# Three pieces moved in the hand-written order of a two-layer transformer kernel's first part

## The reference

```python
h = tok(x, W, b)                                  # patches -> 256 channels
h = concatenate([h, table[x_txt]], axis=1)
h = h + attention(layernorm(h))                   # q.k via a merged wq'wk matrix, causal, softmax, times v
h = h + ternary_down(gelu(ternary_up(rmsnorm(layernorm(h)))))
h = h + recurrent_block(layernorm(h))             # part b
h = h + experts(layernorm(h))                     # part c
```

## Time and profile before

| | us |
|---|---|
| median of 3 runs | 1094.04 (1093.84 to 1098.66) |
| the profiled execution's own time | 1092.31 |
| its span (first to last instruction) | 1090.5 |
| busy TensorE matmul / weight load | 950.0 / 843.3 |
| busy VectorE / ScalarE / GpSimd | 851.2 / 569.7 / 544.4 |
| mean granted TensorE clock, of full speed | 0.945 |

### The profile page before, as it was taken

The page is one execution under the profiler, slowest core; times in us unless marked ns, Lnnn a source line. Parts: engine busy times, 40 slices in busy tenths (PEclk is TensorE's granted clock), DMA queues, the critical chain, the costliest instruction groups (busy, mean ns, idle before and its releaser), DMA issues. The chain is left out here.

```text
span 1090.5 us, 19353 instructions
## 1 busy us (share of the span) xinstructions
PE 950.0 (87%) x5800; PEld 843.3 (77%) x5800; DVE 851.2 (78%) x2471; ACT 569.7 (52%) x1126; POOL 544.4 (50%) x652
## 2 busy tenths in 40 slices
PE   2379999999999999875889999999999999865886
PEld 2268999999999999763567888888888888754675
DVE  2657888888888888861368899989999999845997
ACT  2136555555555555531555676667667667512331
POOL 2126666666666665544134455544455544324553
PEclk9589999999999999977989999999999999966999
DMA  3100311111111132002399999999999999944110
GB/s 140 63 25 26 40 42 45 46 39 50 42 39 39 39 111 74 15 15 82 32 120 136 145 152 154 147 152 155 160 149 152 156 154 134 137 54 166 43 46 20
DMA packets 134814, 96.32 MB, mean 88 GB/s; under 512 B 11208, under 2 KB 129104, under 8 KB 134096
## 3 DMA queue, kind: packets, MB, share of 16 engines
q1 hardware_dynamic: 133200, 91.20, 55.4%
q0 software_dynamic: 1536, 4.20, 1.3%
HBM read 31.92 MB, written 13.11 MB: 41 GB/s over the span
## 5 line engine op out<-in xcount | busy, mean ns | idle before, releaser
L296 POOL TENSOR_TENSOR gelu_lo<-gelu_out,gelu_hi 128x384 fp32r<-128x384 f32 x128 | 152.0, 1206 | 38.9 <-DVE gelu_hi L483 38.1
L897 POOL TENSOR_TENSOR B_decayed_u<-B_scan_in 128x512 f32<-128x512 f32 x48 | 62.0, 1292 | 95.8 <-DMA B_scan_in<-B_stage 93.5
L657 PE MATMUL psA<-ternary_down,gelu_hi 128*128 128x256 f32 x384 | 100.3, 298 | 10.4 <-POOL gelu_lo L296 10.4
L610 PE MATMUL psA<-x2T_hi,ternary_up 128*128 128x384 f32 x256 | 94.0, 367 | 10.5 <-DVE residual L590 10.3
L657 PE MATMUL psA<-ternary_down,gelu_lo 128*128 128x256 f32 x384 | 95.7, 285 | 0.0
L610 PE MATMUL psA<-x2T_lo,ternary_up 128*128 128x384 f32 x256 | 87.8, 343 | 0.0
L657 PEld LDWEIGHTS psA<-ternary_down,gelu_hi 128*128 128x128 f32 x384 | 73.9, 192 | 15.4 <-POOL gelu_lo L296 14.5
L1126 PE MATMUL psB<-Win_hi,B_x_hi 128*128 128x512 f32 x192 | 83.6, 435 | 0.0
L885 POOL TENSOR_TENSOR B_y<-B_scan_in,B_states 128x512 f32<-128x512 f32 x48 | 61.9, 1289 | 43.0 <-ACT B_states L948 43.0
L1138 PEld LDWEIGHTS psB<-B_partial_dots,B_minus_same_batch 128*128 128x128 f32 x384 | 67.2, 196 | 19.8 <-DVE B_partial_dots L1018 8.5
L1034 DVE SCALAR_TENSOR_TENSOR psB<-B_decayed_u,psB 128x128 f32<-128x128 f32 x192 | 68.0, 354 | 13.2 <-PE psB L1138 12.7
(11 more groups left out here) (246 smaller groups left out, 3381.5 us busy)
## 6 DMA issues: line engine op xcount, KB each, us to landing
B_scan_in<-B_stage SPq DMA_DIRECT2D x192, 256.0 KB, 8.1
patches<-in_patches SPq DMA_DIRECT2D x16, 384.0 KB
B_residual<-layer_out SPq DMA_DIRECT2D x48, 128.0 KB, 5.2
out_dram<-B_residual SPq DMA_DIRECT2D x48, 128.0 KB, 4.9
C_raw<-in_experts SPq DMA_DIRECT2D x8, 768.0 KB, 4.6
layer_out<-residual SPq DMA_DIRECT2D x32, 128.0 KB, 1.8
layer_out<-residual SPq DMA_DIRECT2D x32, 64.0 KB, 2.0
weight_stage<-in_upT SPq DMA_DIRECT2D x1, 1024.0 KB, 5.6
```

What stands on the lines that cost most here:

```text
L296: nc.gpsimd.tensor_tensor(act_l[:, k, :], act[:, k % DEEP, :], act_h[:, k, :].bitcast(F32), ALU.subtract).then_inc(s["ffn_lo"], 1)
L610: last = nc.tensor.matmul(out, a, b, start=(n == 0), stop=(n == len(terms) - 1))
L657: last = nc.tensor.matmul(ps[:, 6 + k // 2, (k % 2) * D:(k % 2 + 1) * D], x[:, c, k * P:(k + 1) * P], dn_w[:, c, :], start=(c == 0 and x i ...
L897: nc.gpsimd.tensor_tensor(lu[:, j % 2], ring[:, j % R_RING, :, LAM, :], ring[:, j % R_RING, :, U, :], ALU.mult).then_inc(s["lu"], 1)
```

## The change

Only the list `order` changes. No instruction is added or removed, no wait is changed, `offset` stays.

1. `pT` moves from behind `up.1` to ahead of `up.0`, right behind `tok`.
2. `patch_split` and `patch_load` move from ahead of `emb` to behind `gelu.7`, ahead of `exp_table`, `t` and `h1`; they still work on groups g+3 and g+4.
3. `apply1` moves ahead of `v_split`.

```diff
-        order = """ids_load exp gelu_table tok ternary.0 up.0 up.1 pT patch_split patch_load emb pT_split root1 gelu.0 gelu.1 v
-                v_split apply1 up.2 up.3 gelu.2 add.1 up.4 pv gelu.3 add.2 xT gelu.4 up.5 x_split ternary.1
-                gelu.5 up.6 add.3 up.7 gelu.6 gelu.7 exp_table t h1 root2 gather t_split add.4 add.5
+        order = """ids_load exp gelu_table tok ternary.0 pT up.0 up.1 emb pT_split root1 gelu.0 gelu.1 v
+                apply1 v_split up.2 up.3 gelu.2 add.1 up.4 pv gelu.3 add.2 xT gelu.4 up.5 x_split ternary.1
+                gelu.5 up.6 add.3 up.7 gelu.6 gelu.7 patch_split patch_load exp_table t h1 root2 gather t_split add.4 add.5
                 down.0 down.1 score scale2 add.6 add.7 x2T down.2 max ss x2_split rscale
                 h2.0 h2.1 h2.2""".split()
```

## The result

The changed kernel is slower: median 1114.69 us (1111.31 to 1120.29, 4 runs) against 1095.3 for the kernel before on the same chip, ratio 1.0178 [1.0127, 1.0229]. The forecast was 1098.9, the range 1089 to 1104. The profiled span grew from 1090.5 to 1109.5, by 19.0 us. Nearly all of that is in part a: its last `h2` instruction (line 590) starts at 516.9 instead of 498.3, 18.5 us later.

What follows compares the result with a forecast made beforehand. The prediction took TensorE to bound the step, with the second normalisation nearly level. Twelve steps at +0.5 us and -1.15 us at the ends made +4.85 us, from 1094.04 to 1098.9 us, range 1089 to 1104.

Steps and rivals of the forecast that it cites:

- What bounds the kernel: Part a: TensorE, busy 25.21 of a 26.18 us step, carries it; the second normalisation is nearly level at x2T.
- pT: At up.0: the transposes fill TensorE's 0.64 us wait, and all behind up.1 comes 0.54 us earlier, bounds 0 and 0.64.
- It costs nothing here: VectorE before v_lo: apply1's 1.05 us fills the 0.73 us wait for v_hi; v_lo ends about 246.0, not 246.42.
- The patches' cast: VectorE behind hi.7: the cast follows at once and makes GpSimd's lo.6 wait another 0.47 us.
- The end of the gelus: Casts and subtractions up to lo.7: hi.5 done 1.2 us earlier, lo.7 ends 0.73 us earlier, at 255.11.
- patch_split's new place: GpSimd between lo.7 and root2: the subtraction fills the gap, VectorE's adds delay root2; +0.5 us per step, 0 to +0.8.
- Ends: Steps outside the twelve: step 0 -0.25, step 13 -1.15, step 14 -0.55, step -1 +0.8; together -1.15 us.
- The sum: Whole execution: +6.0 us over twelve steps and -1.15 at the ends, together +4.85 us.
- The slower rival: root2 meets both VectorE adds every step, v_lo is 0.2 us late at pv: +0.8 to +1.0 per step; chance 0.18.

Runs made afterwards that it cites:

- e1: Kernel before with only pT moved ahead of up.0; ratio 0.9946 to the kernel before, step 25.8 us.
- e2: Kernel before with only patch_split and patch_load moved behind gelu.7; ratio 1.0126 to the kernel before, step 27.5 us.
- e3: Kernel before with only apply1 moved ahead of v_split; ratio 1.0106 to the kernel before, step 26.9 us.
- e4: Changed kernel with v_lo ahead of apply1 again, so only pT and patches moved; ratio 1.0069 to the kernel before, step 26.9 us.
- e5: Changed kernel with GpSimd holding lo.0 back until apply1 is done; ratio 1.0054 to the kernel before, step 27.0 us.
- e7: Kernel before with pT ahead of up.0 and add.3 moved behind gelu.6; ratio 1.0054 to the kernel before, step 26.65 us.
- e6: e4 with GpSimd holding lo.6 back until VectorE's patches' cast is done; ratio 1.0118 to the kernel before, step 27.8 us.
- e8: Kernel before with pT ahead of up.0 and only GpSimd's patches' subtraction and load behind gelu.7, cast left ahead of emb; ratio 1.0085, step 27.2 us.

## Why the prediction was wrong

What the argument rests on: the step, the start of `h1` after line 548, and what is left of the step behind that start (means of twelve steps, us).

| | step | `h1` | rest |
|---|---|---|---|
| before | 26.21 | 16.29 | 9.92 |
| changed kernel | 27.60 | 17.67 | 9.93 |
| e1, pT | 25.82 | 15.89 | 9.93 |
| e2, patches | 27.50 | 17.57 | 9.93 |
| e3, apply1 | 26.88 | 16.96 | 9.92 |
| e4, pT and patches | 26.93 | 17.00 | 9.93 |
| e5, lo.0 held | 27.02 | 17.09 | 9.93 |
| e7, add.3 moved | 26.65 | 16.72 | 9.93 |
| e6, lo.6 held | 27.77 | 16.18 | 11.59 |
| e8, subtraction moved | 27.23 | 15.90 | 11.33 |

- **What bounds the kernel**: half right. It named the second normalisation as level with TensorE and as the question of the change. The runs make it stronger: the rest is the same 9.9 in all rows but the last two, so the step moves one for one with the start of `h1`. In e6 and e8 root2 waits for nothing but GpSimd's own subtraction, and that sets the step instead.
- **pT**: right. The wait at `up.0` is gone, `v_hi` starts 3.80 after `up.0` (3.75 forecast). Worth 0.39 a step, not 0.54: with `v_lo` and `apply1` earlier, the latter meets lo.1 (its first instruction takes 0.71 in e1) and the add behind hi.5 waits for lo.4 (1.37).
- **"It costs nothing here" (apply1): the step that failed.** The forecast put `apply1` at 1.05 in its new place, as in the old one, and had `v_lo` end at 246.0, 5.7 after `up.0` starts. It asked whether the inputs were there and whether VectorE had a hole (both came true: `apply1` starts 3.7 after `up.0`, as forecast), and never what runs on GpSimd then. In the new place `apply1` meets lo.0 and lo.1 in full, the three take 2.46, `v_lo` ends 7.1 after `up.0`, and `pv` waits 1.36. Isolated, that is +0.67 a step (e3), and again +0.67 (the changed kernel over e4); over twelve steps 8.0 us. The old place had hidden it: only 0.25 of the first instruction lies beside lo.1. Its row fits an exclusion as well, since it ends at 246.74, 0.16 behind lo.1, as the held ones of the changed kernel do (0.14 and 0.15).
- **The patches' cast: wrong way, and a term mis-sized.** I let it follow hi.7 at once and hold up lo.6 (0.47), because lo.2 had been held up so. Measured: lo.6 went first, the cast took 1.37, `h1` came 1.29 after it. By the Trainium skill, SBUF — State Buffer, section "SBUF: two separate sides", which I had weighed, the subtraction could get in; the trace agrees on that. I priced it by lo.7 alone, and said the moments "aren't late, they come 0.7 earlier". They come 0.7 later even without `apply1` moved (they are there 19.8 after line 548 in e4, 19.1 in the kernel before), and 1.3 later in the changed kernel.
- **The end of the gelus**: wrong. lo.4 ends 11.6 after `up.0` starts, nearly as before (11.7), where the forecast had 10.2; lo.7 ends 16.0 after it instead of 14.8, later than before (15.6) and outside the bounds given (14.3 to 15.3). A late `v_lo` isn't all of it: in e5 `v_lo` ends 5.65 after `up.0`, as forecast, and lo.4 only at 11.2, because the cast, the add and the casts behind `v_lo` now meet lo.1 to lo.3. The forecast had moved them earlier at their present lengths.
- **patch_split's new place**: right in kind and near in size, by another route, so the size is partly luck. pT and patches together cost +0.72 a step (e4), forecast +0.5, bounds 0 to 0.8. The route was root2 held by the patches' subtraction and the adds; in e4 and in the changed kernel root2 waits 0.2 for the moments instead. The meetings of the adds with root2 are real (e6, e8: 0.7) but don't occur in the changed kernel. The loader's wait at `x2T` is 0.65, not 1.5, since TensorE waits elsewhere first.
- **Ends**: -1.15 forecast, +1.9 measured in the profiled execution (18.5 less 16.6 for the twelve steps). Behind the twelve steps it gains 2.1, near the forecast for steps 13 and 14 (-1.7). Ahead of them it loses 4.0 (+0.55 forecast for steps -1 and 0): the first line 548 starts at 110.6 instead of 106.6, with TensorE's mean granted clock at 0.89 instead of 0.94 between 60 and 120 us. How much of the 4.0 is the change's stays open: that start lies between 106.6 and 111.3 over all the runs, at 107.4 in e2 and 111.3 in e8.
- **The sum**: 4.85 forecast, 18.5 measured in part a. The difference of 13.7 is 8.0 from apply1, 2.6 from the 0.22 a step that pT and patches cost more than forecast, and 3.1 from the ends. The slower rival (1102.5 to 1105) had the right sign and too small a price, as `v_lo` was put at 0.2 late.

## What to carry to other kernels

When a piece is moved past work of another engine, ask not only whether its inputs are there and whether its own engine has a hole, but what GpSimd does at that time: an instruction of 0.41 us became one of 1.1 here. Find the chain that moves the step one for one (here `h1`) and read, right in front of it, which instructions take longer than their median; these rows show what to win. Three moves with one plausible reason each should be timed one by one: here the first was a gain of 0.5%, and the other two turned it into a loss of 1.8%.

## What the runs showed of the hardware that was not expected

- `tensor_scalar` with two per-partition scalars, fp32 from SBUF to SBUF, is held up by GpSimd's `tensor_tensor`: 1.11 and 1.10 us beside a subtraction, 0.41 without one, in the same queue order (the changed kernel against e5). Not held up beside such subtractions, in the kernel before, are `v_lo` from PSUM (0.96), line 555 (0.47) and `bn_stats` (0.41). The Trainium skill, VectorE: DVE Perf Modes, section "Mode 2×_2P — use both read ports for one tensor", says that fp32 `tensor_scalar` gets its double rate by reading with both ports. That it is held up fits; the double rate doesn't show: 256 elements take 0.41, as in `bn_stats`, where the cast takes 0.36 for 384. Why the form with two scalars is held up without it isn't shown.
- Who goes first when both sides are waiting isn't settled. In the kernel before, GpSimd's lo.2 is shown from 247.74, while an add ran, and was then held up through cast, add and cast that followed one another (2.27 us instead of 1.02). In the changed kernel lo.6 went ahead of a cast that followed a cast, and in e7 a subtraction went between each two of cast, add and cast.
- A delay can protect: with the late cast (e4, 26.9) the step is shorter than with the cast made early by holding lo.6 (e6, 27.8) or left in its old place (e8, 27.2). In e4 the adds miss root2's small instructions (0.23 each, against 0.54 to 0.62 in the other two).
